# Two-layer cross-attention block: value-tile stores issued by ScalarE instead of SyncE

## The reference

```
# layer 0: 16 heads of 64
x = attn(ln(x, g1, b1), ln(x, g1, b1), Wq1, Wk1, Wv1, Wo1, bo1) + x
x = attn(ln(x, g2, b2), context,       Wq2, Wk2, Wv2, Wo2, bo2) + x
h = ln(x, g3, b3) @ Wp + bp; a, gate = split(h); x = (a * gelu(gate)) @ Wf + bf + x
# layer 1: 16 heads of 16
x = attn(ln(x, n1), ln(x, n1), sq_w, sk_w, sv_w, so_w, so_b) + x
x = gelu(ln(x, n2) @ f1_w1 + f1_b1) @ f1_w2 + f1_b2 + x
x = attn(ln(x, n3), context,   cq_w, ck_w, cv_w, co_w, co_b) + x
x = gelu(ln(x, n4) @ f2_w1 + f2_b1) @ f2_w2 + f2_b2 + x
# attn: q = xq @ Wq, k = xc @ Wk, v = xc @ Wv; softmax(q k^T / sqrt(d)) v, then @ Wo + bo
```

## Time and profile before

| what | us |
|---|---|
| median of 3 runs (lowest, highest) | 4160.89 (4158.42, 4164.56) |
| the profiled execution's own time | 4165.23 |
| its span in the trace | 4163.4 |
| PE busy in the span | 3707.9 (89%) |
| DVE busy | 2495.0 (60%) |
| ACT busy | 2078.6 (50%) |
| POOL busy | 1083.5 (26%) |

### The profile page before, as it was taken

How to read it: one execution, slowest core, us unless ns; L and a number is a source line. 1 busy time by engine, 2 the same in 40 slices (tenths; PEclk the granted TensorE clock), 3 DMA queues, 4 the chain that set the end, 5 groups by cost and what they waited for, 6 DMA issues and landing times. The chain is left out here.

```text
span 4163.4 us, 61859 instructions
## 1 busy us (share of the span) xinstructions
PE 3707.9 (89%) x17468; PEld 2245.6 (54%) x17468; DVE 2495.0 (60%) x4232; ACT 2078.6 (50%) x3669; POOL 1083.5 (26%) x486
## 2 busy tenths in 40 slices
PE   7899977997999999999995887995886999999867
PEld 5644436786555555555544664553664555555455
DVE  4368874332677777777763445763545777777433
ACT  4356653443455555555552333773442666666633
POOL 0056650000566666666660001000002000000000
PEclk9999988998899999999997998997996999999988
DMA  6877758999655555555524325643638444554021
GB/s 214 263 185 194 195 148 311 331 304 288 154 129 128 128 129 128 132 132 132 132 55 144 130 67 99 113 93 136 196 116 165 66 71 69 80 83 77 23 99 40
DMA packets 347831, 591.34 MB, mean 142 GB/s; under 512 B 28584, under 2 KB 181768, under 8 KB 346632
## 3 DMA queue, kind: packets, MB, share of 16 engines
q1 hardware_dynamic: 347656, 589.21, 55.0%
HBM read 349.91 MB, written 239.18 MB: 141 GB/s over the span
## 5 line engine op out<-in xcount | busy, mean ns | idle before, releaser
L1196 DVE TENSOR_REDUCE a_blk_max<-a_mx 128x1 f32<-128x402 f32 (+1 forms) x2560 | 1420.5, 590 | 652.3 <-PE a_mx L999 632.1
L1146 ACT ACTIVATE a_prob<-a_sc 128x512 f32<-128x512 f32 (+1 forms) x2176 | 1225.2, 597 | 775.0 <-PE a_sc L1028 735.1
L999 PE MATMUL a_mx<-a_k_stack,a_q_stack 128*128 128x402 f32 (+3 forms) x2560 | 966.4, 396 | 84.6 <-DMA a_q_stack<-q_lo_cross 24.1
L1039 PE MATMUL a_pv<-a_prob,a_v 128*64 128x512 f32 (+3 forms) x4352 | 876.4, 612 | 0.0
L999 PEld LDWEIGHTS a_mx<-a_k_stack,a_q_stack 128*128 128x128 f32 (+1 forms) x2560 | 501.8, 196 | 475.4 <-DVE a_blk_max L1196 239.5
L975 POOL TENSOR_TENSOR a_prob_sum<-a_prob,a_prob_sum 128x1024 f32<-128x1024 f32 x256 | 617.2, 2412 | 63.3 <-ACT a_prob L1146 53.9
L1028 PE MATMUL a_sc<-a_q_stack,a_k_stack 128*128 128x512 f32 (+1 forms) x1088 | 459.8, 429 | 10.8 <-issue 6.4
L1027 PE MATMUL a_sc<-a_q_stack,a_k_stack 128*128 128x512 f32 (+1 forms) x1088 | 461.4, 424 | 2.1 <-ACT a_q_second L1129 2.1
L1028 PE MATMUL a_sc<-a_q_second,a_k_second 65*128 65x512 f32 (+1 forms) x1088 | 432.7, 398 | 0.0
L975 POOL TENSOR_TENSOR a_prob_sum<-a_prob 128x1024 f32<-128x1024 f32 x128 | 311.9, 2446 | 420.0 <-ACT a_prob L1146 420.0
L740 DVE TENSOR_TENSOR p_split_lo<-p_ps,p_split_hi 128x512 fp32r<-128x512 f32 (+2 forms) x280 | 171.4, 622 | 295.4 <-ACT p_split_hi L628 292.9
(11 more groups left out here) (242 smaller groups left out, 4689.9 us busy)
## 6 DMA issues: line engine op xcount, KB each, us to landing
a_v<-v_cross SPq DMA_DIRECT2D x48, 768.0 KB
a_k_stack<-k_hi_cross SPq DMA_DIRECT2D x32, 801.0 KB, 6.7
a_k_stack<-k_lo_cross SPq DMA_DIRECT2D x32, 801.0 KB, 9.8
a_k_second<-k_hi_cross SPq DMA_DIRECT2D x32, 801.0 KB
v_cross<-p_v_sb SPq DMA_DIRECT2D x48, 512.0 KB, 4.1
k_hi_cross<-p_split_hi SPq DMA_DIRECT2D x120, 200.0 KB, 3.3
k_lo_cross<-p_split_lo SPq DMA_DIRECT2D x120, 200.0 KB, 3.3
a_q_stack<-q_hi_self SPq DMA_DIRECT2D x64, 256.0 KB, 4.8
```

What stands on the lines that cost most here:

```text
L999: nc.tensor.matmul(mx[:, (c * NI + m) % MXB, 0:a.blk], qst[r][0:rows, h, t * P:(t + 1) * P], kst[r][0:rows, h, at:at + a.blk], start=True, ...
L1039: last = nc.tensor.matmul(pv[h * M:(h + 1) * M, :], v[r][0:rows, j, h * M:(h + 1) * M], prob_of(c, cp, h)[0:rows, j % 2, :], start=(j == 0 ...
L1146: nc.scalar.activation(prob_of(c, cp, h)[0:rows, k, :], sc[0:rows, (c * E + e) % SCB, :], ACT.Exp, scale=a.scale).then_inc(exp_done, 1)
L1196: nc.vector.reduce_max(blk_max[:, r, h, t, nb:nb + 1], mx[:, (c * NI + n) % MXB, 0:a.blk], AX.X)\
```

## The change

SP no longer stores value tiles. In its walk through the steps the branch for `v` is gone, and with it the count `ac`. ACT, after the copy (or the two copies) of a `v` tile, waits on its own semaphore `a_read` for the copy to be complete and issues the same DMA itself. Slots, semaphores, sizes and all other orders are the same. In the changed kernel ACT has 120 more rows in its instruction list, SP 142 fewer.

```diff
@@ SP: element(b, steps, more)
-                d = ac = 0
+                d = 0
...
                     elif kind == "k":
                         store_split(b, (kind, m), d, pr.k[a.name], *k_place(m))
-                    elif kind == "v":
-                        sp.wait_ge(a_read, 1 + b * NA + ac + vhalf)
-                        r = a.chunk_rows(m)
-                        dst = pr.v[a.name][bass.ds(b * a.groups_b, a.groups_b), 0:r, m, :]
-                        sp.dma_start(dst.rearrange("g p m -> p g m"),
-                                     v_sb[0:r, m % VPL, :].rearrange("p (g m) -> p g m", m=P))\
-                            .then_inc(v_stored[m % VPL], 16)
                     d += d_tiles(kind)
-                    ac += a_tiles(kind)
@@ ACT: element(b, steps)
                             nc.scalar.copy(dst, src).then_inc(a_read, 1)
+                        act.wait_ge(a_read, 1 + b * NA + ac + vhalf)
+                        dst = pr.v[a.name][bass.ds(b * a.groups_b, a.groups_b), 0:r, m, :]
+                        act.dma_start(dst.rearrange("g p m -> p g m"),
+                                      v_sb[0:r, m % VPL, :].rearrange("p (g m) -> p g m", m=P))\
+                            .then_inc(v_stored[m % VPL], 16)
                     d += d_tiles(kind)
                     ac += a_tiles(kind)
```

## The result

| | before | changed |
|---|---|---|
| median of 5 runs (lowest, highest), us | 4164.56 (4158.42, 4166.26) | 4187.35 (4182.87, 4194.54) |
| the profiled execution's own time, us | 4165.23 | 4189.08 |
| its span, us | 4163.4 | 4187.3 |

The ratio of the times is 1.006, with a 95% interval of 1.0045 to 1.0075: slower by 0.6%, some 23 us. The forecast of 4156.5 and the range up to 4174 both miss it. A later set of 6 runs of the same kernel gave 1.0059 (1.0045 to 1.0073).

What follows compares the result with a forecast made beforehand. It took p1 as bound by DMA bytes and packets, p0 by PE, p2 and p3 by chains between engines. -7.0 + 3.6 - 1.0 = -4.4 us gave 4156.5 against a median of 4160.89; the 8-in-10 range was 4138 to 4174.

Steps and rivals of the forecast that it cites:

- p0, nothing: In p0, no loss: ACT idles 0.77 us before each copy, and SP's 16 issues were not waited for.
- nothing from the order: In p1, no change from the order: bytes same, DMA engines full, ACT's free time covers its issues; phase stays 408 us.
- slower through p1: Rival: in p1, value packets mixed between k packets cost a third of the 39 us bound, +13 us, 4169; chance 0.08.
- p2, -7.0: In p2, earlier value stores free slots sooner: 3.4, 1.4, 1.3 and 0.9 us in four elements, sum 7.0 us gained.
- with the landing time of before: In p2's first element, the early store lands 5.2 us after issue, at 2319.6, so gates start 3.4 us earlier.
- the 1.3 us counted: In p2's third element, two tiles end at 2474.64 against 2475.93, 1.3 us gained.
- p3, +3.6 and -1.0: In p3, ACT starts the shift 1.2 us later in three elements, +3.6 us; the last element's earlier store gains 1.0.
- term 0.85 for a tile: In p2 and p3, one value tile holds ACT for 0.37 + 0.10 + 0.38 = 0.85 us: copy, wait and register instructions, issue.
- 0.95 each, so 0.85 fits between: In p3 behind the shift, four copies took 0.95 us each, so 0.85 per tile fits and only 1.2 us is passed on.
- sharper form: Rival: lower PE clock in p3, twelve gate products, 2.4 to 3.6 us per element; chance 0.12 together with the long issue.
- two of the slower ones: Rivals: value packets in p1, +13 us, chance 0.08; ACT's issue 1.13 us, +11.2, chance 0.12 together with PE's clock.
- What would show it: Signs: p2's second-element gate waits 4.8 us instead of 8.2, p3's gates start 1.2 later, issues last 0.4, p1 stays 408.

Runs made afterwards that it cites:

- the idle copy: Against the kernel before, SP still storing all, ACT waits for each value tile's copy and then makes one idle copy: 4172.00 us, ratio 1.002, p1 406.9.
- the second profile: Profile of the changed kernel measured once more, with nothing altered: median 4188.60 us, ratio 1.0059, p1 421.0, p2 352.5, p3 342.5.
- the two idle copies: Against the kernel before, SP still storing all, in p3 only ACT waits and makes two idle copies behind each value tile: ratio 1.0046, p3 342.1 us.
- GpSimd's queue: Against the kernel before, GpSimd instead of SP issues all value stores on its own queue, ACT neither waiting nor issuing: 4181.66 us, ratio 1.0043.

## Why the prediction was wrong, step by step

*p0, nothing:* right. 195.8 us against 196.4.

*p1, "nothing from the order. The bytes are the same and the DMA engines full":* this step failed first, with +7.6 us in the compared profiles and 13 on average. It priced SP's order only as a delay for value tiles. The order was also the order of service: from two queues a k tile shares the engines with the value tiles beside it, lands 0.5 to 0.9 us later, and its slot, of which there are four, comes free later. That the slots are the way by which this costs time rests on the run with six of them, which left 3.9 us of the loss. ACT's cost was covered there, as the step says (406.9 with the idle copy). The rival "slower through p1" named the sign and the size (+13), but as dearer packets; that price came out at 1.6% (3.06 to 3.11 us per MB) in one stretch. It had 0.08, too little: the rows of before showed 32 us of ACT's waits in this stretch hanging on k stores.

*p2, -7.0:* the early issue came as said, the landing not. The step took 5.2 us "with the landing time of before"; it was 7.3. The store of before went out 3.9 us after the first copy, when o's loads had landed (3.2); issued at 0.55 it stood beside them. Where o landed early, the same early issue landed in 5.3 us. The step also left out what moves up behind the moved store: SP, now free, sent x_from early, and the second store landed later. The third element shows the mechanism undisturbed: the interval fell from 7.66 to 7.18, 0.5 of the 1.3 us counted, and to 6.74 where SP issued the early store. p2 altogether: 352.4 to 354.3 against 351 on average with SP's order, so nothing gained.

*p3, +3.6 and -1.0:* right mechanism, a third of its size (p3 is 12 us longer on average). The term 0.85 for a tile was 1.05: between the copy's end and the issue lie 0.16 us, behind the issue 0.12, where 0.10 was allowed in all. With that the sentence "0.95 each, so 0.85 fits between" tips over: from the start of the shift to the last copy it takes 5.82 us (2956.22 to 2962.04) instead of 5.52 (2943.37 to 2948.89). From tile 6 to the shift it takes 2.1 us instead of 0.5. An element's tiles take 1.9 us longer, not 1.2. The larger part I had named as the "sharper form" of a rival and counted for little: PE waits a little longer and comes out of the wait at the low clock more often, and its busy time grew by 1.0, 1.5 and 4.9 us in the three elements. The gain in the last element didn't come: 32.8 us before and after.

*The rivals:* two of the slower ones came true together, each in another form: p1 lost through slots more than through packets, and ACT's issue wasn't long (0.38, not 1.13), but its surroundings were. The sum of rivals on one side was never taken as a case of its own, so the range ended at 4174. "What would show it" holds for p2's early issue, for the second queue and the 0.4 us of issue, and fails for PE's wait (8.9, not 4.8).

*The Trainium skill.* ACT's issues were 0.38 us at the median and 0.81 at most in p1 and p3 (1.16 in the second profile), beside SP's stretched ones, so the lock on the descriptor generator of which the Trainium skill tells (Perfetto Trace Analysis, "DMA Instruction — HWDGE") cost ACT little there. p0's first issue, 2.66 us from 53.43, doesn't look like it, since SP issued a k store in 0.33 us in its midst, at 53.60; nothing here shows its cause. The Trainium skill (DMA: Bandwidth & Descriptors, "Issuing engines are not separate DMA queues") says that DMAs of several engines interleave on the same 16 DMA engines and that a second issuing engine saves only the sequencer's time. The trace agrees that nothing got faster. It shows beside this that more changed than the sequencer's time: the second engine's transfers were on a queue of their own, the others landed later, and p1 was 13 us longer. Here the measurement decides.

## What to carry to other kernels

When stores leave a full queue for a second one, ask first which of the transfers that stay has few slots: these land later even if bytes and engines are the same. When an engine is relieved, look at the next thing in its stream and what that will collide with. A store that is issued earlier lands earlier only if what it overtook was what held it; here it came in beside loads of 4 MB. And before two profiles are compared interval by interval, look whether the loads ahead of the interval stood at the same place in both. An issue on a compute engine directly behind its own result costs the wait, the issue and both gaps (1.05 us instead of 0.37 here); issued one step later it costs about half of that extra time.

## What I had not expected of the hardware

- The store that ACT issued at 2321.34 moved no packet before 2325, with the other queue full of 2 MB loads until 2323.84 and of stores behind them; from then both queues were served side by side. An issue of 0.38 us says nothing of when its packets move.
- 243 equal products of PE took 55.24 us at a granted clock of 0.95 and 60.18 at 0.89, with PE idle for 13.7 us in that element before and 14.4 after; with the two idle copies the clock was 0.88 at 13.4 us of idle time. So the sum of the pauses doesn't tell the clock. With the clock in p2 (1.00 or 0.87) went whether 4 MB of loads landed 1.9 to 3.2 or 0.3 to 1.6 us after the first value copy, and with that some 2 us of the interval behind it.
- GpSimd's queue moved the same value bytes in 14976 packets (3.5 KB on average) against 103576 on ACT's, and p1 still was no shorter, 422.0 us.
